# One change to a Trainium2 kernel: a buffer of its own for each of 20 pairs of sorted rows, loads issued at once, nine filler products dropped, pair 0 finished earlier

## What is computed

```
x = x + layernorm(attention(layernorm(x)))        # 4 heads of 64, q and k normalised
h = layernorm(x)
scores = h @ gate_w.T                             # 8 experts
chosen = argmax(scores)                           # one expert for each token
x = x + layernorm(h + h @ expert_w[chosen].T)
```

## Time and profile before

| | us |
|---|---|
| three runs | 744.32, 746.66, 750.18 |
| median | 746.66 |
| profiled execution: span from the first to the last instruction | 747.7 |
| PE busy in the span | 620.8 (83%) |
| DVE, ACT, POOL busy | 597.9, 546.2, 291.2 |

### The profile page before, as it was taken

One profiled execution on the slowest core, in us unless ns is written; L12 is line 12 of the kernel. 1 busy time (PEld: TensorE's weight loads), 2 busy tenths in 40 slices (PEclk: granted clock), 3 DMA queues, 4 the chain that ended last, 5 costly groups with the idle time before them and its releaser, 6 DMA issues.

```text
span 747.7 us, 21776 instructions
## 1 busy us (share of the span) xinstructions
PE 620.8 (83%) x8758; PEld 431.1 (58%) x8774; DVE 597.9 (80%) x1145; ACT 546.2 (73%) x878; POOL 291.2 (39%) x457
## 2 busy tenths in 40 slices
PE   4788879999989999857878799999999996277571
PEld 2566636666655666745666366666666675147470
DVE  4998869998889889897898688798888879736462
ACT  3488988888878888764789888788888876325551
POOL 2233435455635543003566332333323211516463
PEclk9899999999999999977999999999999999679885
DMA  5920058988878988121011588889898850244431
GB/s 175 267 74 2 0 100 150 169 166 162 162 140 144 176 157 157 57 82 47 25 34 37 106 160 153 156 149 165 150 164 146 154 128 10 81 139 130 131 100 37
DMA packets 56313, 88.69 MB, mean 119 GB/s; under 512 B 6801, under 2 KB 25492, under 8 KB 56214
## 3 DMA queue, kind: packets, MB, share of 16 engines
q0 software_dynamic: 35088, 66.13, 46.2%
q1 hardware_dynamic: 20550, 21.17, 10.0%
q10 hardware_dynamic: 576, 0.00, 0.0%
HBM read 15.87 MB, written 14.66 MB: 41 GB/s over the span
## 4 chain that ended last, share of the span: by engine, by line
PE 46%; DVE 24%; ACT 10%; DMA 9%; issue 8%; another core or an unknown queue 1%; POOL 0%; SPq 0%; POOLq 0%; DVEq 0%; ACTq 0%
PE banks L1382 15%; PE banks L1232 7%; PE banks L1400 6%; PE banks L1401 6%; PE banks L1402 5%; DVE e_l L998 5%; DMA e_h<-e_f 4%; DMA e_x<-x_all 4%; PE banks L1284 3%; ACT e_f L607 2%; DVE x_all L1055 2%; DVE e_h L842 1%; DVE ss L853 1%; DVE st L1068 1%
## 5 line engine op out<-in xcount | busy, mean ns | idle before, releaser
L998 DVE TENSOR_TENSOR e_l<-e_f,e_h 128x1024 f16<-128x1024 f32 x172 | 212.8, 1263 | 32.5 <-DMA e_h<-e_f 30.5
L607 ACT ACTIVATE e_f<-banks,nbias,c_ 128x1024 f32<-128x1024 f32 x172 | 199.5, 1201 | 42.4 <-PE banks L1382 41.7
L1382 PE MATMUL banks<-q_T,k_T 128*128 128x512 f16 (+1 forms) x1024 | 205.8, 386 | 4.7 <-DVE e_l L872 3.4
L1402 PE MATMUL banks<-v_mm,e_l 128*128 128x65 f16 x2048 | 202.1, 191 | 0.0
L1402 PEld LDWEIGHTS banks<-v_mm,e_l 128*128 128x128 f16 x2048 | 189.8, 99 | 0.0
L1400 PEld LDWEIGHTS banks<-v_mm,e_h 128*128 128x128 f16 x1376 | 126.2, 96 | 42.3 <-DVE e_l L998 21.7
L1400 PE MATMUL banks<-v_mm,e_h 128*128 128x65 f16 x1376 | 137.0, 193 | 7.0 <-DVE attn_x L1010 4.9
L451 POOL DMA_DIRECT2D e_h<-e_f x148 | 79.3, 536 | 154.4 <-ACT e_f L607 144.3
L1401 PE MATMUL banks<-v_mm,e_h 128*128 128x64 f16 x1376 | 136.5, 195 | 0.0
L1401 PEld LDWEIGHTS banks<-v_mm,e_h 128*128 128x128 f16 x1376 | 127.4, 97 | 0.1
L998 DVE TENSOR_TENSOR e_l<-x_all,e_x 128x1024 f16<-128x1024 f32 x84 | 105.9, 1282 | 19.2 <-DMA e_x<-x_all 16.6
(11 more groups left out here) (272 smaller groups left out, 1212.7 us busy)
## 6 DMA issues: line engine op xcount, KB each, us to landing
e_h<-e_f POOLq DMA_DIRECT2D x148, 256.0 KB, 3.8
e_x<-x_all POOLq DMA_DIRECT2D x72, 256.0 KB, 3.9
x_all<-x SPq DMA_DIRECT2D x12, 512.0 KB, 3.8
rows_d<-e_x SPq DMA_DIRECT2D x1, 5180.0 KB, 25.4
k_T<-rows_d SPq DMA_DIRECT2D x20, 259.0 KB, 4.0
x_all<-weT SPq DMA_DIRECT2D x2, 512.0 KB, 10.9
x_all<-weT SPq DMA_DIRECT2D x4, 256.0 KB, 4.3
x_all<-x SPq DMA_DIRECT2D x8, 128.0 KB, 3.5
```

The costliest lines, as they stand in the source:

```text
L607: act.activation(whole[s % ALL % NEF], ps_S[s % ALL % 3], ACT.Exp, bias=bias_of(h, k // NT), scale=CESC).then_inc(s_E, 1)
L998: dve.tensor_tensor(low[s % ALL % NLO], whole[s % ALL % NEF], high[s % ALL % NHI], ALU.subtract).then_inc(s_El, 1)
L1382: ins = pe.matmul(ps_S[s % ALL % 3][:, c * BANK:(c + 1) * BANK], k_T[rows, 1 - c if cross else c, h * N + j * P:h * N + (j + 1) * P], q_T[ ...
L1402: ins = pe.matmul(o, low[s % ALL % NLO][:, at], v[:, 0:DH + 1], start=False, stop=j == NT - 1, skip_group_check=True)
```

## The change

Each of the 20 pairs gets a buffer `rt[q]`: 15 in the memory of `k_T` and 5 in that of `q_T` (both free after attention). The output buffers `ot` move from `k_T` to the memory of `e_l` (four) and behind the row buffers in `q_T` (two). SP loads all pairs one after the other without waiting for outputs. Every wait for a load now is for its own semaphore. `keep_running` reads `e_h16`, and its second block has 2 products instead of 11. DVE does base(1) and finish(0) ahead of low_rows(2). (Lines that only write `rt[q]` for `rt[q % NRT]` are cut.)

```diff
-    NRT, NOT, NU = 8, 6, 4
+    NOT, NU = 6, 4
...
-        at = 0
-        rt = [k32[:, at + i * 2 * RW:at + (i + 1) * 2 * RW].rearrange("p (t d) -> p t d", d=RW) for i in range(NRT)]
-        at += NRT * 2 * RW
-        ot = [k32[:, at + i * 2 * D:at + (i + 1) * 2 * D].rearrange("p (t d) -> p t d", d=D) for i in range(NOT)]
+        q32 = q_T[:, :].bitcast(f32)
+        e_l32 = e_l16.bitcast(f32)
+        IN_K = 2 * H * N // 2 // (2 * RW)
+        homes = [k32[:, i * 2 * RW:(i + 1) * 2 * RW] for i in range(IN_K)]
+        homes += [q32[:, i * 2 * RW:(i + 1) * 2 * RW] for i in range(NPR - IN_K)]
+        rt = [a.rearrange("p (t d) -> p t d", d=RW) for a in homes]
+        ot = [e_l32[:, i * 2 * D:(i + 1) * 2 * D].rearrange("p (t d) -> p t d", d=D) for i in range(4)]
+        at = (NPR - IN_K) * 2 * RW
+        ot += [q32[:, at + i * 2 * D:at + (i + 1) * 2 * D].rearrange("p (t d) -> p t d", d=D) for i in range(NOT - 4)]
...
             sp.wait_ge(s_sc, NB * NT * 16)
             for q in range(NPR):
-                if q >= NRT:
-                    sp.wait_ge(s_o[(q - NRT) % NOT], ((q - NRT) // NOT + 1) * 32)
-                sp.dma_start(rt[q % NRT], rows_d[q * 2 * P:(q + 1) * 2 * P, :].rearrange("(t p) w -> p t w", p=P)).then_inc(s_rt[q % NRT], 16)
+                sp.dma_start(rt[q], rows_d[q * 2 * P:(q + 1) * 2 * P, :].rearrange("(t p) w -> p t w", p=P)).then_inc(s_rt[q], 16)
...
             base(0)
             low_rows(0)
             for q in range(NPR):
+                if q == 1:
+                    base(q)
+                    finish(q - 1)
                 if q + 1 < NPR:
                     low_rows(q + 1)
-                if q:
+                if q > 1:
                     base(q)
                     finish(q - 1)
             finish(NPR - 1)
...
-                    pe.matmul(bank(7), ident16[:, :], q_T[:, 0:BANK], start=True, stop=True)
+                    pe.matmul(bank(7), ident16[:, :], e_h16[:, 0:BANK], start=True, stop=True)
...
             keep_running(12)
             pe.wait_ge(s_sc, NB * NT * 16)
-            keep_running(11)
+            keep_running(2)
             rows_T(0)
```

More of the change, by code:

```diff
@@ L210, in build @@
         s_x, s_small, s_wq, s_wo, s_we, s_init, s_sc = (sem("s_" + n) for n in "x small wq wo we init sc".split())
-        s_rt = [sem(f"s_rt{i}") for i in range(NRT)]
+        s_rt = [sem(f"s_rt{i}") for i in range(NPR)]
         s_o = [sem(f"s_o{i}") for i in range(NOT)]
@@ L464, in _ @@
                     pool.wait_ge(s_fin, 2 * q + t + 1)
-                    pool.indirect_dma_start(out=out_rows, out_offset=bass.IndirectOffsetOnAxis(ap=rt[q % NRT][:, t, D + 2:D + 3].bitcast(u32), axis=0),
+                    pool.indirect_dma_start(out=out_rows, out_offset=bass.IndirectOffsetOnAxis(ap=rt[q][:, t, D + 2:D + 3].bitcast(u32), axis=0),
                                             in_=ot[q % NOT][:, t, :], in_offset=None, bounds_check=NTOK - 1, oob_is_err=False).then_inc(s_o[q % NOT], 16)
@@ L725, in second_base @@
             def second_base(q):
-                act.wait_ge(s_rt[q % NRT], (q // NRT + 1) * 16)
+                act.wait_ge(s_rt[q], 16)
                 if q // NOT * 32 > 0:
                     act.wait_ge(s_o[q % NOT], q // NOT * 32)
-                act.activation(ot[q % NOT][:, 1, :], rt[q % NRT][:, 1, 0:D], ACT.Identity, bias=rt[q % NRT][:, 1, D:D + 1],
-                               scale=rt[q % NRT][:, 1, D + 1:D + 2]).then_inc(s_baseA, 1)
+                act.activation(ot[q % NOT][:, 1, :], rt[q][:, 1, 0:D], ACT.Identity, bias=rt[q][:, 1, D:D + 1],
+                               scale=rt[q][:, 1, D + 1:D + 2]).then_inc(s_baseA, 1)
             high_rows(0)
@@ L1197, in base @@
             def base(q):
-                dve.wait_ge(s_rt[q % NRT], (q // NRT + 1) * 16)
+                dve.wait_ge(s_rt[q], 16)
                 if q // NOT * 32 > 0:
@@ L1201, in base @@
                 for t in range(1 if act_bases(q) else tiles(q)):
-                    dve.tensor_scalar(ot[q % NOT][:, t, :], rt[q % NRT][:, t, 0:D], rt[q % NRT][:, t, D + 1:D + 2], rt[q % NRT][:, t, D:D + 1],
+                    dve.tensor_scalar(ot[q % NOT][:, t, :], rt[q][:, t, 0:D], rt[q][:, t, D + 1:D + 2], rt[q][:, t, D:D + 1],
                                       ALU.mult, ALU.add).then_inc(s_base, 1)
@@ L1504, in keep_running @@
                 for _ in range(count):
-                    pe.matmul(bank(7), ident16[:, :], q_T[:, 0:BANK], start=True, stop=True)
+                    pe.matmul(bank(7), ident16[:, :], e_h16[:, 0:BANK], start=True, stop=True)
             def rows_T(q):
-                pe.wait_ge(s_rt[q % NRT], (q // NRT + 1) * 16)
+                pe.wait_ge(s_rt[q], 16)
                 if q - 1 > 0:
@@ L1512, in rows_T @@
                     for t in range(2):
-                        ins = pe.transpose(ps_TX[q % 2][:, k, t, :], rt[q % NRT][:, t, k * P:(k + 1) * P], ident[:, :])
+                        ins = pe.transpose(ps_TX[q % 2][:, k, t, :], rt[q][:, t, k * P:(k + 1) * P], ident[:, :])
                 ins.then_inc(s_TX, 1)
```

## The result

Over 20 runs each the changed kernel takes 743.67 us (median; 739.21 to 748.81) and the kernel before 747.56 (744.32 to 753.98). The ratio is 0.9953, with a 95% interval of 0.9936 to 0.9971: 3.5 us less, 2.2 to 4.8. That is within 1%, and faster beyond the uncertainty of this measurement. The forecast was 1.9 us less.

The account below looks back on a forecast made before the run. Some five PE pauses, read as coming with POOL's indirect DMAs, fill the expert stage beyond its pair steps. Products -1.9, order 0, loads 0, other buffers 0: 746.66 - 1.9 = 744.8 us, own range 742 to 748, eight in ten 735 to 750.

Parts of the forecast that it names:

- the likeliest class: Whole kernel: time within about 1% (7.5 us) of no change, chance 0.77.
- One sign: Expert stage: 65 to 67 us from first to last pair, listed among what would show the forecast right.
- Nine products, -1.9: PE's block ahead of the transposes: nine products fewer gain 1.9 us, bounds 1.0 and 2.0.
- C: First expert pairs: the shorter block lets PE's granted clock fall back, slowing pairs; 749.3 us, chance 0.08.
- E: Pair 1's load landing behind 663.4 eats the products' 1.9 us: 746.7 us, counted with the forecast.
- The order, 0 with bounds 0 and 1.7: DVE finishing pair 0 ahead of pair 2's low half: POOL starts 1.7 us sooner, worth 0 at the end.
- The loads, 0: Twenty buffers, all loads at once: removes 12 SP waits nobody stands behind, worth 0; possible 0 to -19, +1 or +2.
- The pauses come with POOL's indirect DMAs and not with the loads: Expert stage: PE's some five pauses, about 20 us, come with POOL's indirect DMAs, or at least not with loads.
- Rival A: Expert stage: loads cause the pauses; 726 us if all go, 736 if half, given as 731, chance 0.12.
- B, one pause fewer: Expert stage: output chains are cut otherwise and one 4.2 us pause drops out; 740.6 us, chance 0.14.
- D, loads crowding the outputs: First 7 us of outputs land late and one more pause comes: 749.0, up to 752 us, chance 0.06.

Follow-up runs that it names:

- e9: Kernel before with DVE's new order, POOL holding output 0 until pair 1's first page is finished: ratio 1.0033 to the kernel before.
- e8: Kernel before with DVE's new order and nine products fewer, its 8 buffers and waits kept: ratio 0.9930 to the kernel before.
- e10: e8 with a stop of POOL behind every two outputs: ratio 0.9995 to the kernel before.
- e11: e8 with a stop of POOL behind every four outputs: ratio 0.9922 to the kernel before.
- e4: Changed kernel with its 39 outputs left out, POOL setting one number of a spare buffer instead: 722.93 us, one run.
- e6: Changed kernel with the 39 outputs issued by SP as plain DMAs to a spare table, the result not written: 723.85 us, one run.
- e1: Kernel before with nine products fewer (`keep_running(2)` for `keep_running(11)`), nothing else: ratio 0.9969 to the kernel before.
- e7: Changed kernel with DVE's old order put back: ratio 0.9988 to the kernel before.

## Why the prediction was right, and where not

- *The time* lay in the range, on the right side and in the likeliest class. The gain was put 1.6 us too small (1.9 for 3.5), and the reason is one term. One sign missed with it: I had expected 65 to 67 us from the first to the last pair, and the trace has 63.3.
- *Nine products, -1.9*: right. Alone 2.3 (0.4 to 4.1). In the trace the transposes even come 2.8 us sooner behind the start of the block, since 14 products took 5.07 us and not 5.8: the granted clock rose sooner behind the start of the block (0.62 in the mean over its stretch). Part of that is one execution's luck: over all traces the two kinds of block differ by 2.3 us. Neither the clock nor pair 1's load took it back, so C and E did not occur (the granted clock is 1.00 from 664 to 672).
- *The order, 0 with bounds 0 and 1.7*: this is the step that failed. The lead itself was worked out rightly: the first output comes 1.87 us behind the start of ACT's first root (666.52 to 668.39), where it was 3.60 (670.01 to 673.61), 1.7 sooner. But I valued it at its lower bound, with the reason that "POOL is idle 20 us more after it". The idle time of POOL was no slack: alone the order measured 3.6 (1.9 to 5.2), and with the first output held back (e9) the gain is gone. The upper bound, 1.7, with the 1.9 of the products makes 3.6, about what was measured for the whole (3.5). That the sum meets it so closely is in part luck: alone, the order measured more than its upper bound, and e8, with order and products, 5.2 (3.4 to 7.0).
- *The loads, 0*: right, and for the stated reason. Alone 0.9985 with 1 inside the interval, and order and products without the buffers give 0.9930. No engine waits for a late pair's load in any trace but those with stops put in, which have the 8 buffers of before (e10: PE up to 2.5 us; e11: 0.2).
- *The pauses come with POOL's indirect DMAs and not with the loads*: shown. Without outputs none, with plain outputs none (e4 to e6), with all loads long done they stay (the changed kernel). Rival A is out. The three runs without indexed outputs are one execution each, but all eleven traces with indexed outputs have a wait of ACT of 2.6 us or more in the stage, and none of these three has one above 1.6.
- *B, one pause fewer*: the changed trace has four gaps of PE above 1.2 us where there were five. The sum of the gaps fell by 6.9 us in that pair of traces, and it is smaller in all three kernels with the order and no hold. So something like B did happen, and I had kept it apart from the order's term, though as far as these traces show it is by shorter pauses that the order pays.
- *D, loads crowding the outputs*: not seen. The loads ran until about 677 beside the first outputs, as forecast, at 364 GB/s in all from 670 to 674, and PE's first gap above 1.2 us ends at 686.96, where it was 682.32.

What stays open is the mechanism. ACT waits for transposes or products that the trace shows done 4 to 7 us before (ended 676.84 for the step at 680.85 of the kernel before; about 693.5 for the one at 700.32 of the changed kernel), while POOL issues indexed outputs, and it goes on at about the time at which POOL's chain ends. Something on the way from PE's end to ACT's start is held up; whether it is the increment of the semaphore, the product itself, whose end is only modelled, or ACT, no run here tells. A wait for ACT's own instructions is unlikely for the pause before 700.32: from 697.0 to 700.4 the DMA engines moved 131 packets, all of them POOL's. Nor is it shown that the hold-up is a fixed amount for each output: in e10 and e11 POOL with its stops sets the time, and they cannot tell.

## What to carry to other kernels

An engine that is idle for half of a stage can still set its length, if its instructions hold the others up: before calling its idle time slack, leave its work out once and look whether the others' pauses go. Where pauses stand in a stage, ask what runs in each of them and not only what is waited for; here the loads were the obvious suspect and the outputs the cause. In such a stage an early first output can be worth its lead, and that term should not be put at nothing because the engine is idle later. Stops put in to avoid the pauses brought nothing here that is clear of noise beside the same kernel without them: the longer ones made POOL the engine that sets the time.

## What the runs showed of the hardware

- An indexed output of 128 rows of 1 KB keeps POOL busy for 0.98 us, with 0.30 us to the next, and the stage took 1.6 to 1.8 us for each. A plain one of the same bytes keeps POOL busy for 0.54 us. The kernel took 722.9 us without outputs, 726.3 with plain ones from POOL, 723.9 from SP (one run each) and 743.7 with indexed ones; 19 pairs took 47.5, 50.1, 49.4 and 63.3 us.
- The longest gap of PE, 6.3 us, stands behind the longest chain of indexed outputs, the ten of e9, and with chains of four and stops of 1.5 us no gap is above 1.7. But the length of the chain alone does not fix the gap: behind the first six in a row PE stood 2.7 us in e1 and 4.2 in e7, and in the changed kernel 4.1 us before 718.17 behind four outputs in two pairs.
- 20 loads of 259 KB issued in a row ran at 334 GB/s from 662 to 665 us and, with the first outputs, at 364 from 670 to 674, and PE has no gap above 1.2 us in this time.
